# A feed-forward pipeline of five engines whose groups overlap: the last two second-layer chunks of a group are computed behind the next group's first chunks

## The reference, cut to what matters

```
def _layer(x, ...):
    ...                                   # local attention
    x = x + o @ wo
    h = shift_token(x)                    # second 128 columns come from the token before
    mu = h.mean(-1, keepdims=True)
    var = h.var(-1, keepdims=True)
    h = (h - mu) / jnp.sqrt(var + 1e-05) * lg + lb
    h = h @ w1 + b1                       # 256 -> 2 * 682
    a, g = jnp.split(h, 2, axis=-1)
    h = a * jax.nn.gelu(g, approximate=False)
    x = x + h @ w2 + b2                   # 682 -> 256
    return x
```

## Time and profile before

| | |
|---|---|
| median of 3 runs | 1922.23 us (1918.38 to 1923.25) |
| profiled execution, its own time | 1913.18 us |
| span of its trace | 1911.3 us |
| PE busy | 1668.2 us, 87% of the span |
| DVE busy | 1277.1 us, 67% |
| ACT busy | 908.8 us, 48% |
| POOL busy | 880.7 us, 46% |
| mean TensorE clock granted | 0.945 of full speed |

### The profile page before, as it was taken

How to read it: one execution, slowest core, us unless ns; L and a number is a source line. 1 busy time by engine, 2 the same in 40 slices (tenths; PEclk the granted TensorE clock), 3 DMA queues, 4 the chain that set the end, 5 groups by cost and what they waited for, 6 DMA issues and landing times.

```text
span 1911.3 us, 37856 instructions
## 1 busy us (share of the span) xinstructions
PE 1668.2 (87%) x10522; PEld 1281.6 (67%) x10522; DVE 1277.1 (67%) x3722; ACT 908.8 (48%) x2466; POOL 880.7 (46%) x1070
## 2 busy tenths in 40 slices
PE   3778677999299999999969999399999999789997
PEld 1222365887168778787758788278787887578876
DVE  3666343766488888888655545388888888656765
ACT  1110112544177777777722122177777777711211
POOL 4100022665455555555344544455555555356665
PEclk9888689999699999999989999699999999989998
DMA  4100001121300000000010000200000000001011
GB/s 122 59 1 0 1 0 46 32 67 65 91 3 6 5 5 4 5 4 5 6 60 12 10 7 10 64 4 5 5 4 5 5 4 5 8 23 44 26 40 44
DMA packets 53430, 43.79 MB, mean 23 GB/s; under 512 B 9580, under 2 KB 51840, under 8 KB 53376
## 3 DMA queue, kind: packets, MB, share of 16 engines
q1 hardware_dynamic: 53376, 43.15, 7.2%
HBM read 26.37 MB, written 8.39 MB: 18 GB/s over the span
## 4 chain that ended last, share of the span: by engine, by line
PE 72%; DVE 7%; SPq 5%; DMA 5%; POOL 4%; issue 3%; ACT 2%; POOLq 1%; DVEq 0%; ACTq 0%; PEldq 0%; PEld 0%
PE bank L1445 7%; PE bank L1531 7%; PE bank L1499 6%; PE bank L1458 5%; PE bank L1373 5%; PE bank L1592 5%; PE bank L1593 5%; PE bank L1594 5%; PE bank L1374 5%; PE bank L1375 5%; SPq L465 4%; PE bank L1397 3%; PE bank L1213 3%; DMA x_in<-in_L_attn_hidden_states 2%; POOL h_lo L744 2%
## 5 line engine op out<-in xcount | busy, mean ns | idle before, releaser
L687 POOL TENSOR_TENSOR rnorm<-sumsq,neg_half 128x8 f32<-128x8 f32 x128 | 210.8, 1647 | 202.0 <-DVE sumsq L1940 202.0
L1009 ACT ACTIVATE prob<-prob,neg_max 128x256 f32<-128x256 f32 x512 | 253.7, 500 | 1.5 <-DVE neg_max L2021 1.5
L1126 ACT ACTIVATE gelu_sb<-bank,b_sb 114x512 f32<-114x512 f32 x96 | 66.2, 689 | 350.1 <-PE bank L1594 350.1
L701 POOL TENSOR_TENSOR qk_cos<-qk_cos,qk_sin 128x512 f32<-128x512 f32 x128 | 163.6, 1278 | 133.8 <-DVE qk_cos L1903 133.8
L785 POOL TENSOR_TENSOR act_lo<-act_full,act_hi 114x512 fp32r<-114x512 f32 x96 | 127.0, 1322 | 177.0 <-PE bank L1609 98.1
L1373 PE MATMUL bank<-wqkv_hi,hT_hi 128*128 128x512 f32 x384 | 176.9, 461 | 2.9 <-DVE hT_lo L1889 1.9
L1592 PE MATMUL bank<-h_hi,w_hi 128*114 128x512 f32 (+1 forms) x384 | 156.5, 407 | 20.9 <-POOL h_lo L744 11.0
L2190 DVE SCALAR_TENSOR_TENSOR act_full<-bank,b_sb,gelu_sb 114x512 f32<-114x512 f32 x96 | 71.2, 741 | 124.4 <-PE bank L1594 124.4
L1593 PE MATMUL bank<-h_hi,w_lo 128*114 128x512 f32 (+1 forms) x384 | 153.5, 400 | 0.0
L1375 PE MATMUL bank<-wqkv_hi,hT_lo 128*128 128x512 f32 x384 | 153.2, 399 | 0.0
L1374 PE MATMUL bank<-wqkv_lo,hT_hi 128*128 128x512 f32 x384 | 153.2, 399 | 0.0
(11 more groups left out here) (225 smaller groups left out, 4086.4 us busy)
## 6 DMA issues: line engine op xcount, KB each, us to landing
x_in<-in_L_attn_hidden_states SPq DMA_DIRECT2D x16, 512.0 KB, 3.5
x_scratch<-x_in SPq DMA_DIRECT2D x8, 512.0 KB, 4.2
f_x<-x_scratch SPq DMA_DIRECT2D x8, 512.0 KB, 4.2
out<-f_y SPq DMA_DIRECT2D x8, 512.0 KB, 3.0
hs_attn<-x_sb SPq DMA_DIRECT2D x16, 254.0 KB
hs_ffn<-x_sb SPq DMA_DIRECT2D x64, 63.5 KB
raw<-in_L_ffn_wqkv SPq DMA_DIRECT2D x2, 1536.0 KB, 6.7
raw<-in_L_ffn_w SPq DMA_DIRECT2D x2, 1364.0 KB
```

Source lines behind the costliest of these rows:

```text
L687: pool.tensor_tensor(rnorm[:, part * HEADS:(part + 1) * HEADS], sumsq[:, which * HEADS:(which + 1) * HEADS], neg_half[:, 0:HEADS], ALU.pow ...
L1009: act.activation(prob[:, h], prob[:, h], ACT.Exp, bias=neg_max[:, h:h + 1], scale=-1.0, accum_out=psums[:, h:h + 1]).then_inc(exped, 1)
```

## The change

The last two `down` products of a group are no longer computed at the group's end. PE computes them behind the first two `up` products of the next group: up 0, down 4 of the group before, up 1, down 5 of the group before, up 2, the transposes, down 0, up 3, down 1, up 4, down 2, up 5, down 3. The transposes for the next group stand behind up 2, and no longer behind down 1 of the fourth chunk. The other engines follow:

- DVE adds up the group before at chunk 1 of the next group (new function `add_up`), and normalises the next group at chunk 1, ahead of it, which it did at chunk 2. `last_moments` goes from chunk 1 to chunk 2, `norm_full` from chunk 4 to 3, `last_norm` from chunk 3 to 4.
- POOL makes `h_lo` behind `act_lo` of chunk 3 and no longer at the group's end. `last_root` goes from chunk 2 to 3, and `last_sum` goes behind `act_lo` of chunk 5, where it stood ahead of it.
- ACT makes `h_hi` at chunk 2 (before: chunk 4).
- The first two groups of each stage are written out ahead of the loop, and the last two `down` products and the last `add_up` stand behind it. Waits that only later chunks had (`j >= 2`, `j >= 3`) now hold for every chunk but those of the first group.

```diff
@@ POOL
-                        if j == 2 and before:
+                        if j == 3 and before:
                             last_root(g - 1, 1 - i)
-                        if j == 5 and before:
-                            last_sum(g - 1, 1 - i, u + i)
                         pool.wait_ge(act_hi_ready, FC * k + j + 1)
-                        if j >= 3:
+                        if j >= 3 or not first:
                             pool.wait_ge(w2_used, FC * k + j - 2)
                         ...
-                    norm_lo(n0 + g + 1, 1 - i)
+                        if j == 3:
+                            norm_lo(n0 + g + 1, 1 - i)
+                        if j == 5 and before:
+                            last_sum(g - 1, 1 - i, u + i)
@@ ACT
-                            if j == 4:
+                        if j == 2:
                                 norm_hi(...)
@@ PE
+                def group(u, i, first):
+                    k = lay * NG + u * 2 + i
+                    n = n0 + u * 2 + i
+                    pe.wait_ge(nT_lo, 1 + 2 * n + 2)
+                    for j in range(FC):
+                        up(k, j, i, first)
+                        if j == 2:
+                            turn_norm(n + 1)
+                        if j >= 2:
+                            down(k, j - 2)
+                        elif not first:
+                            down(k - 1, j + FC - 2)
...
-                        for j in range(FC + 2):
-                            if j < FC:
-                                up(k, j, i)
-                            if j >= 2:
-                                down(k, j - 2)
-                            if j == 3:
-                                turn_norm(n + 1)
+                for j in range(FC - 2, FC):
+                    down(lay * NG + NG - 1, j)
@@ DVE
+                def add_up(k, g):
+
+                    dve.wait_ge(w2_used, FC * (k + 1))
+                    dve.wait_ge(b2_added, k + 1)
+                    for h in range(2):
+                        xs = x_sb[:, bass.ds(g * GB + 2 * h, 2), :]
+                        dve.tensor_tensor(xs, bank[:, 4 + h].rearrange("p (b d) -> p b d", d=D), xs, ALU.add).then_inc(x_ffn, 1)
...
-                        if j == 1 and before:
+                        if j == 1:
+                            norm_apply(n, (g + 1) % NG)
+                            if not first:
+                                add_up(k - 1, g - 1)
+                        if j == 2 and before:
                             last_moments(g - 1, 1 - i)
-                        if j == 2:
-                            norm_apply(n, (g + 1) % NG)
-                        if j == 3 and before:
+                        if j == 3:
+                            norm_full(n)
+                        if j == 4 and before:
                             last_norm(g - 1, 1 - i, u + i)
-                        if j == 4:
-                            norm_full(n)
```

More of the change, by code:

```diff
@@ L763, in last_sum, with group @@
                     pool.tensor_tensor(f_y[:, i], f_y[:, i], f_x1[:, i], ALU.add).then_inc(f_sum, 1)
-                def group(u, i, before):
+                def group(u, i, first, before):
                     g = u * 2 + i
@@ L785, in group @@
                         pool.tensor_tensor(act_lo[0:w, j % 3], act_full[0:w, j % 2], act_hi[0:w, j % 3], ALU.subtract).then_inc(act_lo_ready, 1)
-                    norm_lo(n0 + g + 1, 1 - i)
[L788 to L791, removed]
+                        if j == 3:
+                            norm_lo(n0 + g + 1, 1 - i)
+                        if j == 5 and before:
+                            last_sum(g - 1, 1 - i, u + i)
+                last = lay + 1 == DEPTH
+                group(0, 0, True, False)
+                group(0, 1, False, last)
+                with pool.Fori(0, NG // 2 - 1) as u:
+                    for i in range(2):
+                        group(u + 1, i, False, last)
+                if not last:
                     end_phase(pool, 7 + 4 * lay)
                 else:
[L794 to L798, removed]
                     last_root(NG - 1, 1)
@@ L1117, in _ @@
                 end_phase(act, 6 + 4 * lay)
-                with act.Fori(0, NG // 2) as u:
-                    for i in range(2):
[L1120 to L1123, removed]
-                            if j >= 2:
-                                act.wait_ge(act_ready, FC * k + j - 1)
-                            act.activation(gelu_sb[0:w, j % 2], bank[0:w, j % 2], ACT.Gelu, bias=b1_sb[0:w, 1, j:j + 1]).then_inc(g_ready, 1)
-                            if j == 4:
[L1128 to L1133, removed]
+                def group(u, i, first):
+                    k = lay * NG + u * 2 + i
+                    for j in range(FC):
+                        w = fw(j)
+                        act.wait_ge(g_ps, FC * k + j + 1)
+                        if j >= 2 or not first:
+                            act.wait_ge(act_ready, FC * k + j - 1)
+                        act.activation(gelu_sb[0:w, j % 2], bank[0:w, j % 2], ACT.Gelu, bias=b1_sb[0:w, 1, j:j + 1]).then_inc(g_ready, 1)
+                        if j == 2:
+                            norm_hi(n0 + u * 2 + i + 1, 1 - i)
+                        if i == 0 and j == 5 and lay + 1 < DEPTH:
+                            act.wait_ge(raw_attn, 16 * (lay + 2))
+                            act.activation(wqkv_hi[:, :, bass.ds(u * SHARE, SHARE)], raw[:, 0:2, bass.ds(u * SHARE, SHARE)],
+                                           ACT.Copy).then_inc(split_hi, 1)
+                for i in range(2):
+                    group(0, i, i == 0)
+                with act.Fori(0, NG // 2 - 1) as u:
+                    for i in range(2):
+                        group(u + 1, i, False)
                 if lay + 1 < DEPTH:
@@ L2210, in group @@
                                           wqkv_hi[:, :, bass.ds(u * SHARE, SHARE)], ALU.subtract)
[L2211 to L2220, removed]
+                last = lay + 1 == DEPTH
+                group(0, 0, True, False)
+                group(0, 1, False, last)
+                with dve.Fori(0, NG // 2 - 1) as u:
+                    for i in range(2):
+                        group(u + 1, i, False, last)
+                add_up(lay * NG + NG - 1, NG - 1)
+                if not last:
                     end_phase(dve, 7 + 4 * lay)
                 else:
[L2223 to L2227, removed]
                     dve.wait_ge(x_ffn, 1 + 2 * NG * DEPTH)
```

20 lines of the change are left out of this document (11 added, 9 removed).

## The result

The changed kernel takes 1934.89 us (median of 5 runs, 1932.49 to 1936.38), the kernel before 1922.23 (5 runs, 1918.38 to 1925.13). The ratio is 1.0077, with a 95% interval of 1.0061 to 1.0093. The forecast was 1929, range 1912 to 1938: the direction was right and its size half of what came.

A forecast was written before the change was run, and what follows sets the result against it. PE bounds the kernel, losing 1.36 us per group to a serial chain ending in `h_lo`. Boundaries -4.0, +3.6 and -0.55, first groups +6.0, clock +1.8: +6.9 on 1922.2 gives 1929 us, range 1912 to 1938.

The forecast's parts named there:

- what goes: Group boundaries: PE's loss around late `h_lo` and `act_lo` 5 vanishes, 1.36 us each, 0.52 more at three first-layer boundaries.
- what is late next: Chunk 1 onward: transposes wait for `hn` (0.3 us in the first layer), then `down 0` for `add_up` (about 0.45).
- First layer: First-layer stage: boundaries gain 4 x 0.55 + 3 x 0.6 = 4.0 us; its first group loses 3.0 waiting at the transposes.
- list of signs: Expected trace: transposes waiting 0.3, 1.4 and 3.0 us, pitches 26.9 to 27.2 in the first layer, 28.0 in the second.
- `act_hi` of chunk 0 slips in between: Second layer: DVE's cast runs between POOL's `last_sum` and `b2`; transposes 1.44 us late, +0.6 per group in groups 2 to 7.
- first rival: Second layer: POOL's `b2` goes ahead of `act_hi` 0, transposes 2.6 us late, +7, 1936 us; chance 14%.
- My argument for the forecast: Against `b2` going first: at 1802.05 the waiting engine, POOL, got in between two `hn`.
- The rule that I set against the change: VectorE and GpSimd share ports exclusively; the first to issue blocks the other for an instruction, so `act_hi` can now wait.
- The clock: PE in the stages: new waits invite falls to 1.2 GHz; one more on balance, +1.8 us, bounds -1.8 and +7.2.
- The sum: Both stages: -4.0 + 3.6 - 0.55 + 6.0 + 1.8 = +6.9 us, giving 1929.
- second rival: Chunk 1: `hn` starts ahead of `act_lo` 1 and is in time; together -14 us, 1908; chance 17%.
- the third: Second layer: POOL is not the bound and it behaves as the first; 7 us less than forecast, 1922; chance 27%.

The follow-up runs named there:

- three moves: Changed kernel with `b2` added behind chunk 2, additions ahead of `hn`, transposes and `h_hi` in chunk 3: 1895.73 us, ratio 0.9887.
- one move each: Changed kernel with only `b2` behind chunk 2 (1917.80 us), only additions ahead of `hn` (1932.28), or only transposes and `h_hi` in chunk 3 (1944.40).
- `b2` halves: Changed kernel with POOL's addition of `b2` as two instructions of 512 columns instead of one of 1024: 1936.53 us, ratio 1.0105.
- `last_sum` ahead: Changed kernel with `last_sum` on POOL ahead of `act_lo` of chunk 5 again: 1923.01 us, ratio 1.0023.
- `b2` later: Changed kernel with POOL adding `b2` behind `act_lo` of chunk 2 instead of ahead of chunk 0: 1917.80 us, ratio 1.0000.
- additions first: Changed kernel with DVE adding up the group before ahead of the eight `hn`: 1932.28 us, ratio 1.0062.
- transposes later: Changed kernel with the transposes and `h_hi` back in chunk 3, behind down 1: 1944.40 us, ratio 1.0157.
- two moves: Changed kernel with additions ahead of `hn`, transposes and `h_hi` in chunk 3, `b2` left in place: 1895.22 us, ratio 0.9884.
- `h_lo` earlier, no overlap: Kernel before with POOL's `h_lo` behind `act_lo` of chunk 4 and `last_sum` behind `act_lo` 5: 1904.67 us, ratio 0.9918.

## Why the prediction came out as it did

**Right: what goes.** The wait for `h_lo`, with its 1.36 us per boundary and 0.52 more behind `wqkv_lo`, is gone, as the trace of the changed kernel shows. The kernel with three moves has a pitch of 26.13 us, which is PE's own work of 26.1 as read from the earlier trace rows, in the groups written out ahead of the loop as in the others, so those cost nothing, as taken.

**Right: what is late next.** The transposes wait for `hn` in every group. `down 0` waits for the additions in 13 of the 14 groups behind the first ones, forecast at 0.4 to 0.45 us; it starts 0.35 us later than it would (0.38 us behind the last transpose instead of 0.03). The kernels with one move each and the one with all three show that there was nothing else.

**First layer.** Forecast -4.0 at the boundaries and +3.0 in the first group, without the clock -1.0 us; the stage measured -0.9. That the two agree so well is in part luck of the clock. The fall of before at 1086 no longer appears, which is worth 1.6 us (the pitch of that group was 29.04 and not 27.47). Against it, the lower level at the stage's beginning lasts 5.95 us instead of 3.32, which costs at most 1.3. Without both the stage is 0.6 us shorter, not 1.0. The boundaries gained less than forecast: over groups 1 to 6 the pitches fell by 2.9 us in all (that fall left out), where the sum has 3.45. The pitch is 27.3, as the transposes wait 0.58 us, not 0.3. The prediction's list of signs gave 26.9 to 27.2, but its own sum gives 26.9 and, behind `wqkv_lo`, 27.4 (27.99 less 0.6). In groups 2 to 7 the root ends after `act_hi` 1, so that the first `hn` is late even ahead of being held. The wait in the first group was 2.37, and 2.64 in the second layer, forecast 3.0.

**The step that failed: "`act_hi` of chunk 0 slips in between".** In the second layer I let the cast in between `last_sum` and `b2`, with 0.6 us lost per group as the outcome. It stands outside for the whole of `b2`. The first rival had this case at 14%, with the transposes 2.6 us late and 1936 as its time; measured were 2.35 us from where PE was ready, and 1934.9. Its chain is the one that ran: in us of the group, moments at 8.7, root at 10.35, `act_lo` 1 at 11.6, `hn` at 13.5, where it had 8.75, 10.4, 11.7 and 13.8. That its time came out so near is again partly luck: the boundaries cost less than it had, the clock more. My argument for the forecast was that POOL at 1802.05 had got in between two `hn`. That was a row on POOL waiting for DVE, and I used it for DVE waiting for POOL. The `hn` ahead of the held one shows it:

```profile
1801.99 0.34 DVE L2134 TENSOR_SCALAR hn<-x_sb,mv,rstd 128x128 f32 x1
```

`act_lo` starts 0.06 us behind it, takes 1.43 instead of 1.30, and goes ahead of the next `hn`. The halves show that the two directions differ. The rule that I set against the change (the Trainium skill, "SBUF — State Buffer", "Who interferes with whom": whoever issues first holds the pair of ports for a whole instruction) is borne out by the trace, 2.66 us for a cast of 0.43. It deserved to carry more than 14%, because both sides of that race were within 0.1 us of each other by my own times (3.8 and 3.83).

**The clock.** I took +1.8 us. By the record of the granted clock, PE was at 1.2 GHz for 10.2 us of the two stages before and for 26.8 after, which is at most 8.3 us of time. The second layer lost 5.7 to the falls in groups 3 to 6, which came behind the waits of 2.18 us. Had the waits stayed at the forecast 1.4, there would likely have been fewer. No run has such waits; the nearest are 0.91, with no fall in six, 1.56, with none in two, and 1.77, with two in six.

**The sum.** Stages: forecast +6.9, measured +17.4 in the profiled execution. The excess is in the second layer, +18.3 instead of the +6.05 that it had without the clock. Its seven boundaries cost some 8.1 us instead of 3.05, the falls in groups 3 to 6 another 5.7, and the first group together with the stage's end 4.5 instead of 3.0, with a fall of the clock in it. The measured time lies inside the range because the range took in the first rival. The ratio of the runs gives 0.77% of 1922, 14.8 us, and the medians 12.7. For the eight experiments the stages and the ratios agree within 3 us, as they do here:

| kernel | stages, less before | ratio x 1922 us |
|---|---|---|
| changed | +17.4 | +14.8 |
| `last_sum` ahead | +5.1 | +4.4 |
| `b2` later | -1.4 | 0.0 |
| `b2` halves | +19.9 | +20.2 |
| additions first | +13.9 | +11.9 |
| transposes later | +30.1 | +30.2 |
| three moves | -19.6 | -21.7 |
| two moves | -20.5 | -22.3 |
| `h_lo` earlier, no overlap | -13.5 | -15.8 |

**The other side.** The second rival (`hn` in time, 1908) did not come: in the changed kernel one `hn` is held in every group, for 1.1 to 1.4 us. Nor did the third (1922): the second layer did not behave as the first, its pitch is 28.89 and not 27.3.

**Open.** The profiled execution of before began its first stage 5.4 us earlier than that of the changed kernel, behind phases that both have in common. This goes with the clock and not with the change: PE was at 1.2 GHz there for 147 us before and 168 after. In the ten profiled executions the stage began at 969.8 to 974.3 us where that was 140 to 153 us, and at 978.7 to 979.4 where it was 168 to 176, in the kernel before with `h_lo` earlier too. What sets the clock there stays open. Nor does any run explain why POOL's next instruction goes ahead of a waiting one of DVE.

## What to carry to other kernels

When work is overlapped across a boundary, lay out for each wait of the bounding engine the time at which it now asks and the time at which the chain behind it ends; here the end of a chain of six steps on two engines had been asked for at 14 us of the group, which did no harm, and was now asked for at 11. Before restructuring, look at what stands last in the old order: moving `h_lo` (and `last_sum` with it) gave 16 of the 22 us. The good overlap needed two edits together (additions first, transposes later): alone, one made the changed kernel slower by 0.8% and the other moved it by 0.15%, within the noise, and both together made it faster by 2%, so such parts are not judged one at a time.

## What the runs showed of the hardware

- A VectorE cast (512 columns, 0.43 us) that becomes ready 0.02 to 0.03 us after a GpSimd addition has begun is held until its end: 2.66 us for one instruction of 1024 columns, 2.81 for two of 512. GpSimd's second instruction went ahead of the waiting cast, in six groups of six.
- In the other direction GpSimd does get in: `act_lo` at 1802.05 started during one `hn`, took 1.43 us instead of 1.30, and held the next `hn` for 1.33 instead of 0.33.
- How often PE's clock fell from 2.4 to 1.2 GHz behind an idle time of a given length, inside the stages:

| idle time of PE before it | cases | falls |
|---|---|---|
| 0.64 to 0.78 us, at the transposes (additions first) | 8 | 0 |
| 0.78 to 0.80 us, at the first `up` (kernel before) | 14 | 1 |
| 0.82 to 0.92 us, at the transposes (`last_sum` ahead) | 6 | 0 |
| 1.56 us, at `down 0` (transposes later) | 2 | 0 |
| 1.77 us, at `down 0` (transposes later) | 6 | 2 |
| 2.18 to 2.19 us, at the transposes (changed; additions first) | 12 | 8 |
| 2.32 to 2.34 us, at the transposes (`b2` halves) | 6 | 5 |
| 2.36 to 2.41 us, at the transposes of a first group | 3 | 0 |
| 2.64 to 2.65 us, at the transposes of a first group | 7 | 5 |
| 3.4 us, at `down 0` (transposes later) | 6 | 6 |

The length of the idle time alone does not decide it: the same 2.18 us were followed by a fall in some groups of one execution and not in others. Where a group without a fall stands beside it, a fall cost 1.2 to 1.6 us.
